# Packing the causal score blocks of a row-maximum pass into full PSUM banks

## What is computed

```python
q = q * cos + rotate_half(q) * sin          # 16 heads, 16 wide; k the same
scores = einsum('bhqd,bhkd->bhqk', q, k) * HEAD_DIM ** -0.5
scores = where(causal, -inf, scores)        # causal: key after query
attn = softmax(scores, axis=-1)
out = einsum('bhqk,bhkd->bhqd', attn, v)
```

## Time and profile before

| what | value |
|---|---|
| median of three runs | 3074.97 us |
| profiled execution, its own time | 3059.91 us |
| its span, first to last instruction | 3058.1 us |
| PE busy | 2735.0 us, 89% of the span |
| DVE busy | 1885.7 us, 62% |
| ACT busy | 1213.5 us, 40% |
| POOL busy | 749.8 us, 25% |
| granted TensorE clock, mean | 0.922 of full speed |

### The profile page before, as it was taken

The page is one execution under the profiler, slowest core; times in us unless marked ns, Lnnn a source line. Parts: engine busy times, 40 slices in busy tenths (PEclk is TensorE's granted clock), DMA queues, the critical chain, the costliest instruction groups (busy, mean ns, idle before and its releaser), DMA issues.

```text
span 3058.1 us, 45977 instructions
## 1 busy us (share of the span) xinstructions
PE 2735.0 (89%) x15374; PEld 1735.1 (57%) x15374; DVE 1885.7 (62%) x5534; ACT 1213.5 (40%) x2706; POOL 749.8 (25%) x1279
## 2 busy tenths in 40 slices
PE   4885899899998999899998999989998999989996
PEld 3663566456655666466655566566664666555544
DVE  5443666665667556666667666675566666666652
ACT  1321244454434444444434343343444444343352
POOL 2321232223222222213322232222322133221111
PEclk7986899999999999899899999999999999999998
DMA  2024103311232213411134112332134111343211
GB/s 58 1 62 112 22 17 95 95 40 40 59 102 74 53 25 95 122 40 39 40 86 123 39 37 61 87 89 52 26 86 120 47 42 36 83 116 78 58 36 45
DMA packets 137424, 193.99 MB, mean 63 GB/s; under 512 B 49439, under 2 KB 111214, under 8 KB 127854
## 3 DMA queue, kind: packets, MB, share of 16 engines
q1 hardware_dynamic: 131808, 190.89, 24.6%
q10 hardware_dynamic: 5390, 0.18, 0.1%
HBM read 122.34 MB, written 67.63 MB: 62 GB/s over the span
## 4 chain that ended last, share of the span: by engine, by line
PE 68%; DVE 15%; DMA 3%; issue 3%; ACT 2%; POOL 1%; SPq 1%; DVEq 0%; ACTq 0%; POOLq 0%
PE bank L735 10%; PE bank L768 8%; PE bank L749 8%; PE bank L664 4%; PE bank L571 4%; PE bank L502 3%; PE bank L551 3%; PE bank L678 3%; PE bank L511 3%; PE bank L520 3%; PE bank L665 3%; DVE bank L1087 3%; DVE mxa L1090 2%; PE bank L481 2%; PE bank L606 2%
## 5 line engine op out<-in xcount | busy, mean ns | idle before, releaser
L1290 ACT ACTIVATE pexp<-bank 128x512 f32<-128x512 f32 (+3 forms) x1536 | 674.7, 495 | 605.3 <-PE bank L749 603.6
L735 PE MATMUL bank<-stk,stq 128*128 128x512 f32 (+3 forms) x1536 | 632.1, 426 | 121.5 <-DVE mxa L1087 33.2
L1087 DVE CUSTOM_DVE_ANT_0 bank<-bank,maskneg 128x128 f32<-128x128 f32 (+3 forms) x1024 | 501.5, 497 | 376.8 <-PE bank L735 371.2
L735 PEld LDWEIGHTS bank<-stk,stq 128*128 128x128 f32 x1536 | 305.4, 201 | 502.1 <-issue 449.7
L749 PE MATMUL bank<-stq,stk 128*128 128x512 f32 (+3 forms) x1536 | 535.6, 422 | 55.3 <-ACT pexp L1290 51.3
L1090 DVE TENSOR_REDUCE mxa<-bank 128x1 f32<-128x512 f32 x512 | 351.8, 687 | 159.7 <-PE bank L735 154.1
L1438 POOL TENSOR_SCALAR_AFFINE_SELECT pexp<-pexp 128x256 f32<-128x256 f32 x512 | 211.6, 419 | 786.9 <-ACT pexp L1290 786.8
L749 PEld LDWEIGHTS bank<-stq,stk 128*128 128x128 f32 x1536 | 281.2, 202 | 196.7 <-ACT pexp L1290 121.6
L768 PE MATMUL bank<-pexp,vsm 128*32 128x512 f32 (+3 forms) x3072 | 360.2, 543 | 8.1 <-POOL pexp L1438 7.7
L1356 POOL TENSOR_SCALAR_AFFINE_SELECT arena<-arena 128x512 f32<-128x512 f32 x128 | 79.4, 644 | 411.2 <-ACT arena L1194 411.2
L571 PE MATMUL bank<-arena 32*128 32x256 f32 x1024 | 155.6, 423 | 15.6 <-DVE arena L895 11.1
(11 more groups left out here) (183 smaller groups left out, 4170.7 us busy)
## 6 DMA issues: line engine op xcount, KB each, us to landing
stq<-q_halves SPq DMA_DIRECT2D x128, 256.0 KB
arena<-rope_table SPq DMA_DIRECT2D x8, 2048.0 KB
q_halves<-arena SPq DMA_DIRECT2D x32, 512.0 KB, 2.9
k_halves<-arena SPq DMA_DIRECT2D x32, 512.0 KB, 2.8
stk<-k_halves SPq DMA_DIRECT2D x64, 256.0 KB
stk<-k_halves SPq DMA_DIRECT2D x128, 128.0 KB
v_rows<-arena SPq DMA_DIRECT2D x16, 544.0 KB, 4.1
vsm<-v_rows SPq DMA_DIRECT2D x16, 544.0 KB, 3.8
```

Of the source, the lines that this page charges most:

```text
L735: mm(bk[:, 0:k1 - k0], stq[b_][:, h % 2, qb * P:(qb + 1) * P], stk[b_][:, h % 2, k0:k1], start=True, stop=True).then_inc(s["r_full"], 1)
L1087: nc.vector.tensor_tensor_reduce(out=sc, in0=sc, in1=maskneg[:, CH - (k1 - k0):CH], scale=1.0, scalar=LOWEST, op0=ALU.add, op1=ALU.max, ac ...
L1290: nc.scalar.activation(pexp[:, u % NPX, j, 0:n], ps(j)[:, 0:n], ACT.Exp, scale=DK ** -0.5).then_inc(s["exp_done"], 1)
```

## The change

The 12 blocks of a head are put into 9 uses of the ring ("packs"), each of exactly 512 columns. Three packs hold two blocks, six hold one. The blocks, their matmuls and their reductions stay what they are; PE signals after the last matmul of a pack, and DVE frees the bank after the last reduction of a pack. A group has 36 uses. They are spread over the 24 steps as one use (part 0) in the steps with `values` and two uses (parts 0 and 1) in the other steps.

```diff
-        sunits = [(h, qb, k0, min(P * (qb + 1), k0 + CH)) for h in range(G) for qb in range(NT)
-                  for k0 in range(0, P * (qb + 1), CH)]
+        packs = (((0, 0), (2, 0)), ((3, 0),), ((1, 0), (5, CH)), ((4, 0),), ((4, CH), (6, CH)), ((5, 0),), ((6, 0),), ((7, 0),),
+                 ((7, CH),))
+        sunits = []
+        for h in range(G):
+            for pack in packs:
+                col, blocks = 0, []
+                for qb, k0 in pack:
+                    n = min(P * (qb + 1), k0 + CH) - k0
+                    blocks.append((qb, k0, n, col))
+                    col += n
+                sunits.append((h, blocks))
...
-            score_at[SX - LEAD + n // 2, n % 2] = divmod(n, NSU)
-        max_tr_at = {SX - LEAD + NSU // 2 * (g + 1) + 1: g for g in range(NG * NB)}
+            score_at[SX - LEAD + n // 3 * 2 + (n % 3 + 1) // 2, n % 3 // 2] = divmod(n, NSU)
+        max_tr_at = {SX - LEAD + NTU * (g + 1) + 1: g for g in range(NG * NB)}
...
-                    mm(bk[:, 0:k1 - k0], stq[b_][:, h % 2, qb * P:(qb + 1) * P], stk[b_][:, h % 2, k0:k1],
-                       start=True, stop=True).then_inc(s["r_full"], 1)
+                    for qb, k0, n, col in blocks:
+                        last = mm(bk[:, col:col + n], stq[b_][:, h % 2, qb * P:(qb + 1) * P], stk[b_][:, h % 2, k0:k0 + n],
+                                  start=True, stop=True)
+                    last.then_inc(s["r_full"], 1)
...
-                        sc = r_bank("s", g, i)[:, 0:k1 - k0]
-                        if k1 == P * (qb + 1):
-                            nc.vector.tensor_tensor_reduce(out=sc, in0=sc, in1=maskneg[:, CH - (k1 - k0):CH], scale=1.0, scalar=LOWEST,
-                                                           op0=ALU.add, op1=ALU.max, accum_out=dst).then_inc(s["r_used"], 1)
-                        else:
-                            nc.vector.reduce_max(dst, sc, AX).then_inc(s["r_used"], 1)
+                        for qb, k0, n, col in blocks:
+                            dst = mxa[:, g % 2, NT * h + qb:NT * h + qb + 1] if k0 == 0 else mxb[:, g % 2, 4 * h + qb - 4:4 * h + qb - 3]
+                            sc = r_bank("s", g, i)[:, col:col + n]
+                            if k0 + n == P * (qb + 1):
+                                last = nc.vector.tensor_tensor_reduce(out=sc, in0=sc, in1=maskneg[:, CH - n:CH], scale=1.0, scalar=LOWEST,
+                                                                      op0=ALU.add, op1=ALU.max, accum_out=dst)
+                            else:
+                                last = nc.vector.reduce_max(dst, sc, AX)
+                        last.then_inc(s["r_used"], 1)
...
-                    at = SX - LEAD + n * NSU // 4 - 4
+                    at = SX - LEAD + n * NTU // 2 - 4
```

More of the change, by code:

```diff
@@ L729, in score @@
                 def score(g, i):
-                    h, qb, k0, k1 = sunits[i]
+                    h, blocks = sunits[i]
                     b_ = slot(g, h // 2)
@@ L1081, in core_dve @@
                         g, i = score_at[t, part]
-                        h, qb, k0, k1 = sunits[i]
-                        dst = mxa[:, g % 2, NT * h + qb:NT * h + qb + 1] if k0 == 0 else mxb[:, g % 2, 4 * h + qb - 4:4 * h + qb - 3]
+                        h, blocks = sunits[i]
                         r_filled(nc.vector, "s", g, i)
-                        sc = r_bank("s", g, i)[:, 0:k1 - k0]
-                        if k1 == P * (qb + 1):
-                            nc.vector.tensor_tensor_reduce(out=sc, in0=sc, in1=maskneg[:, CH - (k1 - k0):CH], scale=1.0, scalar=LOWEST,
-                                                           op0=ALU.add, op1=ALU.max, accum_out=dst).then_inc(s["r_used"], 1)
-                        else:
-                            nc.vector.reduce_max(dst, sc, AX).then_inc(s["r_used"], 1)
+                        for qb, k0, n, col in blocks:
[7 more added lines that the diff above has]
+                        last.then_inc(s["r_used"], 1)
                         if i == NSU - 1:
```

## The result

| | before | after |
|---|---|---|
| median, runs side by side | 3070.43 us (4 runs) | 3028.93 us (4 runs, 3022.91 to 3035.37) |
| profiled execution | 3059.91 us | 3027.61 us |
| its span | 3058.1 us | 3025.9 us |
| granted TensorE clock, mean | 0.922 | 0.928 |

The ratio is **0.9869, 95% interval 0.9834 to 0.9904**: faster by 1.3%. A second measurement of the same two kernels gave 0.9847 (0.9826 to 0.9867). The forecast was 3055 us with a range of 3012 to 3088: the result is inside the range, but the gain was twice the one summed.

What follows compares the result with a forecast made beforehand. PE's fixed work plus its standing time was taken as the bound. Small stalls 18 plus hidden waits 9 less transposes 7 gave 20 us off 3075.0, so 3055 us; range 3012 to 3088 for 8 in 10.

Steps and rivals of the forecast that it cites:

- What bounds the kernel: PE's fixed work plus its standing time sets the time; PE has work in 89% of the span, DVE 62%.
- The walks: Large stalls followed step by step on PE and DVE: net 0 and +0.30 us, taken as 0 in the sum.
- second walk: At the 0.93 us stall, the second score use without `values` waits for a two-block pack: a 0.30 us loss.
- The ring's transposes: Transposes of lines 785 and 791, which share the ring, wait for longer reads: 7 us lost.
- Small stalls: A third of the scores' 82.2 us waits for DVE, 27 us; two of three positions relieved: 18 us gained.
- at the tight v positions nothing goes: Scores in steps with `values` still wait for the last other step's first use, as before: no gain there.
- first walk: Through the 1.54 and 1.23 us stalls: 0.45 us won, the rest waits one place later; net about nothing.
- Hidden waits: Waits inside stretched 512-column score matmuls, 0 to 26 us: middle 13 taken, two thirds relieved, 9 us gained.
- handoffs: Ring uses fall from 1536 to 1152; nothing taken as saved on DVE or on PE.
- The clock: PE's mean granted clock, expected between 0.92 and 0.93; a rise above 0.935 would show the forecast wrong.
- the clock holds as well: Rival: less standing keeps PE at 2.4 GHz, 48 us on top of 20, so 3007 us; chance 0.18.
- DVE busy: DVE's busy time in the profile after the change was to stay within 10 us of 1885.7.

Runs made afterwards that it cites:

- e4: Kernel before the change, with PE waiting for its loaded operands only at the first use after a load, not at every use: 3064.45 us, ratio 0.9961.
- e5: Changed kernel, with PE waiting for its loaded operands only at the first use after a load, not at every use: 3013.91 us, ratio 0.9797.
- e6: Changed kernel, with all two-block packs moved to the second use in the steps without `values`: 3005.49 us, ratio 0.9788.
- e8: Changed kernel, with two uses in the steps with `values` and one in the other steps: 3007.57 us, ratio 0.9795.
- e7: Changed kernel, with all two-block packs moved to the first use in the steps without `values`: 3030.14 us, ratio 0.986.
- e2: Changed kernel, with the first block of each two-block pack also incrementing a semaphore nobody waits for, 384 increments more: 3025.2 us, ratio 0.9839.
- e1: Changed kernel, with PE repeating the two already satisfied waits ahead of the second block of each two-block pack: 3022.93 us, ratio 0.9829.

## Why the prediction was right in sign and short in size

- **What bounds the kernel** was right: PE. In the stretches above that are wholly at half clock it is busy for 9.1 to 10.2 of 10.2 us.
- **The walks** held. Against the score that waits in v, the transposes of line 490 were forecast 1701.46 - 1697.64 = 3.82 us later and line 663's matmuls 1704.92 - 1697.64 = 7.28 us later; they came after 1683.29 - 1679.55 = 3.74 and 7.32 us. Line 663 comes 9.85 us after the start of the layer norm's statistics, where line 654 came 1704.92 - 1695.08 = 9.84 us after it: it landed where it was. In v 1.37 us are stood where the walk had 1.54 - 0.45 = 1.09 left, and of the stall of 1.23 us 0.52 was left where I had none. At the second walk's place the stall is at the second use of o, as forecast:

```profile
1944.75 0.47 PE L745 MATMUL bank<-stk,stq 128*128 128x256 f32 x2 [1.20 <-DVE mxa L1099]
```

  1.20 us in place of 0.93: a loss of 0.27 us, 0.30 forecast.
- **The ring's transposes**, -7 us: measured 26.4 - 18.7 = 7.7 us more waiting.
- **Small stalls, +18 us**: mis-sized. The scores' waits fell by 9.3 us, not by 18 ("50 to 65 us" was 72.9), and with the transposes' 7.7 almost nothing of that is left in PE's idle time, which was to fall by some 20 us and went from 323.1 to 326.5. The step that was wrong is "at the tight v positions nothing goes". The uses of o were relieved by more than 18 us, from 55.3 to 30.5 us of waits, nearly all of the first use's and a fifth of the second's. But v waits 15.6 us more, 42.4 in place of 26.8: the first walk had said of one stall that its rest waits one place later, and the sum didn't carry that over to the others. That most waits would stand in v was forecast and came true (60 of 100).
- **Hidden waits, +9 us**: the part that came. The rest without the clock is 10 to 23 us while the shown waits fell by 1.6 us net, so 8 to 21 us lie in what the profile counts as durations. The prediction valued **handoffs** at nothing; by e4's and e5's traces some 2.5 us are theirs, inside the waits' fall. So the sum of 20 us stands beside 10 to 23 measured, of another make than I had written it; that the two numbers agree is in part luck.
- **The clock** was the step that failed. The sum held it still, and the term that is missing is the 22 to 34 us that went with it, against 48 us in the rival "the clock holds as well", whose case (2985 to 3035 us) is the one that came true, with a chance of 0.18. My reason against it was that the clock only falls behind the large stalls, and that these stay. They do stay; but a stall of 1.42 us became one of 1.25 us, and three of four batches shown kept their clock. It is a stall of line 749 for ACT, of which the prediction had said that the change doesn't touch it. "Near the edge", which the prediction itself had read from the earlier trace rows, was worth more than one rival. The clock that the prediction expected to see, 0.92 to 0.93, is the one that came (0.928 in the profile, 0.930 in the mean), so its own sign of being wrong, a clock above 0.935, could not show the miss: from 0.9197 to 0.9301 the step is worth as much as the whole forecast gain.
- **DVE busy** fell by 27 us (1885.7 to 1858.7), where I had said within 10. The durations of DVE's instructions add up to 2202.6 us before and 2216.7 after, but they overlap by 358.0 us in place of 316.9: the second read of a pack begins before the first has ended, and no longer waits for PE. Ahead of the reads of 384 keys DVE stood idle for 126.0 us before; now:

```profile
L1099 DVE CUSTOM_DVE_ANT_0 bank<-bank,maskneg 128x384 f32<-128x384 f32 x256 | 153.0, 598 | 0.0
```

  So "on DVE nothing is saved" had been read from the places where banks are full, and most were not. On an engine that isn't the bound this shows no gain of its own.

What stays open is what decides whether the clock falls behind a given stall: length alone does not, since it got worse behind 2.15 us where 2.27 us had stood. The split into 22 to 34 and 10 to 23 us is worked out from the scatter of measured clocks; no run here held the clock fixed. The clock may itself answer to the standing that the change took away, and e6 and e8 show only that it can rise without the product falling.

## What to carry to other kernels

Before explaining a small gain by waits, set the span of every execution against its mean granted clock: here that told that about half of a 1.5% gain, perhaps three quarters, went with the clock. A wait that is taken away at one place has to be looked for at the next: here 25 us less at two uses stood against 16 us more at the third. Where banks of a ring are the meeting point of two engines, judge the unit and the order together: the order alone cost 98 us here (3070.5 to 3168.4), and the larger unit gave back 143. A place at which the clock falls in some batches and not in others is cheap to move; try several placements of the same work and keep the best, rather than reason about which waits they remove (of three tried here on the changed kernel, e6 and e8 gained and e7 didn't).

## What the runs showed of the hardware that was not expected

- The clock's fall behind one and the same place of the program differs from batch to batch in one execution (0.50, 0.50, 0.67, 0.50 before; 0.50, 1.00, 1.00, 1.00 after), and the clock goes with most of the scatter of the whole kernel's time, spans of 3057.3 to 3089.5 us.
- A semaphore increment on a matmul between two others costs nothing that 384 of them would show (e2), nor do satisfied waits at the same place (e1). A second, satisfied wait ahead of one that really stands costs 0.09 us each time: the matmul starts 0.135 us after the semaphore's update with it and 0.043 us without (before against e4, after against e5); about 1470 such waits, of which 135 fell on a score that stood, cost 0.4%.
- The first matmul behind those of `values` costs about 0.1 us more than elsewhere, a narrow one and a wide one alike (to the start of the next, at 128 columns 0.163 against 0.060 us, at 512 columns 0.337 against 0.234).
- Twice as many waits for ACT, with 25 us more in all, went together with a higher clock (e8: 0.9385 against 0.9301).
